# Writing the attention mask into PSUM with ScalarE, and moving the second half's scores

## The chip, the cores and the metric

The kernel runs on one core of one Trainium2 chip. The metric is device time in microseconds (us). The engines work from instruction streams of their own and meet at semaphores: TensorE (PE in the profile; its weight loads are PEld), VectorE (DVE), ScalarE (ACT), GpSimd (POOL), and SyncE (SP), which here only issues transfers (DMAs).

## The reference, cut to what matters

The program has four stages; the last one is six layers of local attention and a gated feed-forward net on 16 sequences of 256 tokens with 128 channels. The change concerns the scores of the local attention (16 heads, windows of 32 tokens, each of which sees its own window and the one before, so 64 keys):

```
mask = (it < jb) | (it > jb + w) | (jb == -1)
sim = einsum('bhwie,bhwje->bhwij', bq, bk2) * 8.0
sim = where(mask, -finfo.max, sim)
attn = softmax(sim, -1)
out = einsum('bhwij,bhwje->bhwie', attn, bv2)
```

In the kernel the banned places are 0 / -1e30 in a constant `mask_bf`, which the scores are added to.

## The kernel before, in words

The last stage (`phase_d_*`) runs 96 sequence-steps (6 layers by 16 sequences) as a software pipeline. Each engine has a hand-written loop over turns `f` (100 of them, `TURNS_D`), and each turn works on several sequences in different phases: sequence `f` is transposed, split and projected (chunks 0 to 4), `f-1` gets its chunks 5 to 7, its rotary products, norms and the placing of keys and queries, `f-2` its scores, softmax and token products, `f-3` the weighted sum (`attention`) and the start of the feed-forward net, `f-4` the rest of that net. The order on each engine is written out by hand; nothing is reordered.

The parts that matter here, by name and line:

- `scores(n, h)` on PE (L1915), once for each half `h` of a sequence, fills two PSUM banks, 2 and 3. For each bank it first puts the mask there by four products of `ident_bf` with `mask_bf` (L1923, one for each 32 rows, 512 columns, bf16), with `start=True`, and then adds 32 score products (L1930, `start=False`). It waits for the placed keys and queries (`s_dk`, `s_dq`) and for the subtraction that last read the banks (`s_sub`).
- On DVE `softmax_maximum` (L1470) and `softmax_shift` (L1476) read banks 2 and 3; the second signals `s_sub`. `rotary_products` (L1428) works on the projected chunks. `split_low_tokens` is L1416, `residual` L1503, `ffn_gate` L1529, `scale_keys` L1464.
- On ACT `squares` (L1660) reads each projected chunk, `softmax_exp` is L1676, `read_products` L1684, `ffn_gelu` L1723, and in three turns of each layer it also converts weights and makes tables (L1732, L1744, L1753).
- On POOL `rotary_sums` (L1815) adds the two rotary products, `add_halves` (L1823) adds squares, `scale_shifted` (L1832) scales the shifted scores, `softmax_scale` (L1838) the probabilities.
- On SP `place_queries` (L2141) and then `place_keys` (L2132) issue eight transfers each, SBUF to SBUF, for every sequence. The queries wait for the last rotary sum (`s_ad`), the keys for `scale_keys` (`s_mR`). The next sequence's first rotary sum waits until the keys have landed (`s_dk`, L1813), since it writes what they are read from.

PE's order in a turn: transpose tokens, up-projection of `f-4`, scores half 0, project 5, attention half 0, project 6, up-projection, project 7, scores half 1, `sum_squares` (L1901), attention half 1, token products (L1957) with projections 0 to 4 and the other work between them. The rings: a projected chunk's bank is free again when the rotary product two chunks back has been made (`s_rp`), and a rotary product's buffer when the rotary sum three chunks back is done (`s_ad`).

Of the kernel before, what the change touches and what calls it, by code (L numbers as in the profile page):

```python
# [20 lines left out]
ACT = mybir.ActivationFunctionType  # L21
# [50 lines left out]
def build(nc, dram, out):  # L72
    ctx = ExitStack()
    with ctx:
# [1094 lines left out]
        def phase_c_tensor(pe):  # L1169
# [86 lines left out]
            def sequence_turns(n, s, left):  # L1256
# [59 lines left out]
        tab_flat = tab[:, :, :, :, :].rearrange("p m k h t -> p (m k h t)")  # L1316
        base_stage = tab_flat[:, 4 * TPS * DH:4 * TPS * DH + 4 * TPS * P].rearrange("p (k t r f) -> p k t r f", k=4, t=TPS, r=4)

        (s_sel, s_basep, s_base, s_zk, s_normed, s_zero, s_stats, kept,
         s_xtp, s_xt, s_split, s_proj, s_sq, s_sa, s_xh, s_rp, s_ad, s_sm, s_y, s_r, s_zh, s_z, s_rq, s_R, s_mR, s_dk, s_dq,  # L1320
         s_s, s_sub, s_rm, s_exp, s_inv, s_prob, s_pt, s_u, s_uev, s_at, s_x2, s_x2p, s_xf, s_mean, s_xsq, s_var,
         d_chain, d_act_chain, s_y2, s_xc, s_xn, s_up, s_gl, s_h, s_ffo, s_x_done, s_m, s_mvo, s_whi, s_wlo, s_tab,
         loaded_qk, loaded_sc, loaded_vo, loaded_w1, loaded_w2) = (
            sem("d_" + s) for s in (
                "sel basep base zk normed zero stats kept "
                "xtp xt split proj sq sa xh rp ad sm y r zh z rq R mR dk dq "
                "s sub rm exp inv prob pt u uev at x2 x2p xf mean xsq var "
                "chain act_chain y2 xc xn up gl h ffo x_done m mvo whi wlo tab "
                "loaded_qk loaded_sc loaded_vo loaded_w1 loaded_w2").split())
        back = [sem(f"d_back{g}") for g in range(4)]  # L1330
        KEEP = NT // len(back)
        kept_in = wqk_stage[:, :].rearrange("p (g n c) -> p g n c", g=2, c=C)
        x_kept = [kept_in[:, 0], kept_in[:, 1], wvt[:, :, :], wo[:, :, :]]
        STORES = ((0, 4), (4, 8), (8, 12), (12, 15), (15, 16))
        ZEROS = 5
        TURNS_D = TOTAL + 4

        def at_least(eng, s, count):

            if count >= 1:  # L1340
                eng.wait_ge(s, count)
# [64 lines left out]
        def phase_d_vector(dve):  # L1406
# [116 lines left out]
            def ffn_gate(n, c):  # L1523
                if not here(n):
                    return
                m = FBLK[c]
                dve.wait_ge(s_gl, NF * n + c + 1)
                at_least(dve, s_ffo, n)
                nc.vector.scalar_tensor_tensor(d_h[0:m, c, :], bank[UP_BANK[c]][0:m, T:2 * T], cols_of(n)[0:m, 2 + c:3 + c],  # L1529
                                               d_gl[0:m, c % 2, :], ALU.add, ALU.mult).then_inc(s_h, 1)  # L1530
# [51 lines left out]
            for f in range(TURNS_D):  # L1582
                turn_probabilities(f - 3, 1)
                rotary_products(f - 1, 3)
                ffn_gate(f - 4, 0)
                rotary_products(f - 1, 4)
                softmax_maximum(f - 2, 0)
                rotary_products(f - 1, 5)
                softmax_shift(f - 2, 0)
                rotary_products(f - 1, 6, 7)  # L1590
                ffn_gate(f - 4, 1)
                softmax_maximum(f - 2, 1)
                split_low_tokens(f)
                ffn_gate(f - 4, 2)
                norm_weight(f - 1)
                residual(f - 3)
                norm_factor(f - 1)
                rotary_products(f, 0)
                norm_split(f - 1)
                softmax_shift(f - 2, 1)  # L1600
                scale_keys(f - 1, 0)
                rotary_products(f, 1)
                scale_keys(f - 1, 1)
                softmax_sum(f - 2, 0)
                rotary_products(f, 2)
                ffn_weight(f - 3)
                softmax_reciprocal(f - 2, 0)
                ffn_factor(f - 3)
                ffn_scale(f - 3)
                softmax_sum(f - 2, 1)  # L1610
                softmax_reciprocal(f - 2, 1)
                if f - 4 == LAST:
                    add_kept(3, SEQS - 4, SEQS - 1)
                ffn_residual(f - 4)
                turn_factors(f - 1)
                turn_probabilities(f - 2, 0)
                if f < 2:
                    normalise(*range(3 + 7 * f, min(10 + 7 * f, SEQS)))
                done = f - 4 - SEQS * (LAYERS - 1)
                if done > 0 and done % 4 == 0:  # L1620
                    add_kept(done // 4 - 1, done - 4, done)
# [3 lines left out]
        def phase_d_scalar(act):  # L1625
# [36 lines left out]
            def norm_rsqrt(n):  # L1662
                if not here(n):
                    return
                act.wait_ge(s_sm, 2 * n + 2)
                at_least(act, s_z, n)
                at_least(act, s_rq, n)
                link(nc.scalar.activation(d_y, bank[7][:, 0:T], ACT.Ln, bias=1e-24))
                link(nc.scalar.activation(d_y, d_y, ACT.Exp, scale=-0.5))
                nc.scalar.activation(d_w, d_y, ACT.Square).then_inc(s_y, 1)  # L1670

            def softmax_exp(n, h):
                if not here(n):
# [89 lines left out]
            for f in range(TURNS_D):  # L1763
                fresh = here(f) and f % SEQS == 0
                next_fresh = here(f + 1) and (f + 1) % SEQS == 0
                read_products(f - 3, 7)
                read_tokens(f)
                split_high_tokens(f)
                nc.scalar.preload_act_table(ACT.Gelu)
                ffn_gelu(f - 4, 0)  # L1770
                squares(f - 1, 5, 6)
                ffn_gelu(f - 4, 1)
                squares(f - 1, 7)
                ffn_gelu(f - 4, 2)
                nc.scalar.preload_act_table_set(EXP_SET)
                norm_rsqrt(f - 1)
                if fresh:
                    tables(layer_of(f), 0)
                softmax_exp(f - 2, 0)
                if here(f - 2) and (f - 2) % SEQS == 0:  # L1780
                    head_matrices(layer_of(f - 2))
                squares(f, 0)
                norm_high(f - 1)
                read_products(f - 2, 0, 1, 2)
                squares(f, 1)
                if fresh and f:
                    weights_high(layer_of(f), 4, 5, 6, 7)
                ffn_tokens(f - 3)
                read_products(f - 2, 3)
                ffn_square(f - 3)  # L1790
                read_products(f - 2, 4)
                squares(f, 2, 3)
                if fresh:
                    tables(layer_of(f), 1)
                if next_fresh:
                    weights_high(layer_of(f + 1), 0, 1, 2, 3)
                ffn_rsqrt(f - 3)
                softmax_exp(f - 2, 1)
                read_products(f - 2, 5)
                ffn_shift(f - 3)  # L1800
                squares(f, 4)
                read_products(f - 2, 6)


        def phase_d_gpsimd(pool):
# [32 lines left out]
                nc.gpsimd.tensor_tensor(d_e[h], d_e[h], d_inv[h].unsqueeze(2).to_broadcast([P, 4 * QUADS, 2 * WIN]), ALU.mult)\  # L1838
                    .then_inc(s_prob, 1)

            nc.gpsimd.memset(d_k, 0.0).then_inc(s_zk, 1)
            nc.gpsimd.memset(d_u[:, 0], 0.0).then_inc(s_zk, 1)
            for f in range(TURNS_D):
                fresh = here(f) and f and f % SEQS == 0
                next_fresh = here(f + 1) and (f + 1) % SEQS == 0
# [18 lines left out]
        def phase_d_tensor(pe):  # L1864
# [50 lines left out]
            def scores(n, h):  # L1915
                if not here(n):
                    return
                pe.wait_ge(s_dk, 128 * (n + 1))
                pe.wait_ge(s_dq, 128 * (n + 1))
                at_least(pe, s_sub, 2 * n + h)  # L1920
                for b in range(2):
                    for g in range(4):
                        nc.tensor.matmul(bank[2 + b][g * WIN:(g + 1) * WIN, :], ident_bf[:, g * WIN:(g + 1) * WIN],  # L1923
                                         mask_bf[:, min(h + b, 1), :, :].rearrange("p a k -> p (a k)"),
                                         start=True, stop=True, skip_group_check=True, tile_position=(0, g * WIN))
                    for v in range(2):
                        at = (4 * h + 2 * b + v) * WIN
                        for a in range(2):
                            for g in range(4):
                                last = nc.tensor.matmul(bank[2 + b][g * WIN:(g + 1) * WIN, (2 * v + a) * P:(2 * v + a + 1) * P],  # L1930
                                                        d_q[:, a, g, at:at + WIN], d_k[:, a, g, :, at:at + 2 * WIN],
                                                        start=False, stop=True, skip_group_check=True, tile_position=(0, g * WIN))
                last.then_inc(s_s, 1)
# [119 lines left out]
                last.then_inc(s_basep, 1)  # L2053
            pe.wait_ge(s_base, 4)
            pe.wait_ge(s_zero, ZEROS)
            pe.wait_ge(s_zk, 2)
            for f in range(TURNS_D):
                if f == 1:
                    pe.wait_ge(s_stats, 13)
# [6 lines left out]
                project(f - 1, 6)  # L2066
                ffn_up(f - 4, 2)
                project(f - 1, 7)
                scores(f - 2, 1)
                sum_squares(f - 1, 1)  # L2070
                attention(f - 3, 1)
                if here(f - 2) and (f - 2) % SEQS == 0:
                    head_matrices(layer_of(f - 2), 0, 1, 2, 3)
                token_products(f - 2, 0)
# [302 lines left out]
```

## Time and profile before

| | |
|---|---|
| runs | 4246.09 us median of 3 (4245.45 to 4252.16) |
| profiled execution | span 4245.4 us from the first to the last instruction, mean granted TensorE clock 0.965 |
| share of the span that each engine is busy | PE 92%, DVE 84%, ACT 62%, POOL 56% |
| last stage | about 1330 us to the end, 100 turns |
| two steady turns (PE's transposes of one turn to those of the next) | 29.21 us each |

The profile gives for the profiled execution its span; its own time is not listed apart from that. Busy shares are averages over four stages; the last stage has to be read by itself.

### The profile page before, as it was taken

Reading aid. Unit: us, or ns where it says so; the run is one execution under the profiler, and the core shown is the slowest. Engines: PE = TensorE matmul, PEld = TensorE weight load, DVE = VectorE, ACT = ScalarE, POOL = GpSimd, SP = SyncE. Lnnn points to the kernel's source line nnn. Section 1 sums busy time; section 2 is a strip of 40 time slices with the busy share of each in tenths; the row PEclk is TensorE's granted clock in tenths of the full one; section 3 lists DMA queues with packets and bytes.
Section 4 is the critical chain, followed back from the end, with each engine's and each line's share of the span. In section 5 each row is a group of like instructions: output and inputs, shape, how many; then the busy total and the mean of one; then the engine's idle time right before and its main releaser. Section 6 shows DMA issues by size and latency. Waiting matters only on the chain.

```text
span 4245.4 us, 120089 instructions
## 1 busy us (share of the span) xinstructions
PE 3898.6 (92%) x48128; PEld 2739.2 (65%) x48128; DVE 3566.7 (84%) x5529; ACT 2619.0 (62%) x5518; POOL 2380.4 (56%) x2045
## 2 busy tenths in 40 slices
PE   3457998999995999999999999999999999999998
PEld 1225776777774676667766676667766676667675
DVE  7986556777776899989998899989998899989897
ACT  2442335666664666666667666666666666666665
POOL 0111001000002787878888788878878787878785
PEclk7668999999997999999999999999999999999999
DMA  3000000000001333233332333233332333333332
GB/s 104 0 0 1 1 1 1 1 0 0 0 1 40 71 95 81 64 80 88 79 76 67 77 90 81 68 76 88 79 77 66 75 92 81 69 76 70 93 75 68
DMA packets 264482, 238.94 MB, mean 56 GB/s; under 512 B 31524, under 2 KB 260136, under 8 KB 263208
## 3 DMA queue, kind: packets, MB, share of 16 engines
q1 hardware_dynamic: 263976, 231.82, 23.4%
q8 instruction: 363, 5.95, 0.6%
q14 instruction: 143, 1.17, 0.1%
HBM read 26.20 MB, written 4.19 MB: 7 GB/s over the span
## 4 chain that ended last, share of the span: by engine, by line
PE 72%; DVE 13%; ACT 7%; issue 3%; SPq 2%; POOL 1%; DMA 1%; DVEq 0%; ACTq 0%; POOLq 0%
PE bank L1957 14%; PE bank L1890 13%; PE bank L1975 8%; PE bank L1930 7%; PE bank L2017 5%; PE bank L834 4%; ACT arena L1109 3%; PE bank L2030 2%; PE bank L1923 2%; DVE arena L996 2%; PE bank L1901 2%; DVE arena L1006 2%; PE bank L1234 1%; PE bank L1225 1%; PE bank L1912 1%
## 5 line engine op out<-in xcount | busy, mean ns | idle before, releaser
L1428 DVE TENSOR_TENSOR arena<-bank,tab 128x1024 f32<-128x1024 f32 x768 | 936.5, 1220 | 187.5 <-ACT arena L1660 136.0
L1815 POOL TENSOR_TENSOR arena<-arena 128x512 f32<-128x512 f32 x768 | 1009.8, 1330 | 47.4 <-DMA arena<-arena 43.2
L1660 ACT ACTIVATE arena<-bank 128x512 f32<-128x512 f32 x768 | 458.1, 597 | 537.8 <-PE bank L1890 527.8
L1957 PE MATMUL bank<-m_vo,arena 128*32 128x512 f32 x6144 | 757.6, 599 | 17.3 <-DVE arena L1521 11.0
L1890 PE MATMUL bank<-x_split,wqk_split 128*128 128x256 f32 x4608 | 720.1, 299 | 35.0 <-DVE arena L1428 21.0
L1890 PEld LDWEIGHTS bank<-x_split,wqk_split 128*128 128x128 f32 x4608 | 605.1, 191 | 183.9 <-issue 94.3
L1823 POOL TENSOR_TENSOR arena<-arena 128x256 f32<-128x256 f32 x768 | 556.7, 736 | 162.4 <-ACT arena L1660 161.9
L1684 ACT ACTIVATE arena<-bank 128x512 f32<-128x512 f32 x768 | 456.4, 595 | 187.4 <-PE bank L1957 184.7
L1832 POOL TENSOR_TENSOR arena<-arena 128x1024 f32<-128x1024 f32 x192 | 371.6, 1936 | 261.0 <-DVE arena L1476 261.0
L1167 POOL TENSOR_TENSOR x_all<-x_all,arena 128x256 f32<-128x256 f32 x16 | 11.6, 726 | 833.8 <-DVE arena L988 833.8
L1838 POOL TENSOR_TENSOR arena<-arena 128x1024 f32<-128x1024 f32 x192 | 373.4, 1945 | 127.3 <-DVE arena L1489 127.0
L1930 PE MATMUL bank<-arena 128*32 128x128 f32 x12288 | 403.0, 273 | 0.6 <-issue 0.6
L1975 PE MATMUL bank<-arena 128*32 128x128 f32 x12288 | 373.7, 274 | 0.0
L1930 PEld LDWEIGHTS bank<-arena 128*32 128x32 f32 x12288 | 345.1, 110 | 37.5 <-issue 1.2
L1975 PEld LDWEIGHTS bank<-arena 128*32 128x32 f32 x12288 | 333.1, 110 | 31.4 <-issue 0.7
L1957 PEld LDWEIGHTS bank<-m_vo,arena 128*32 128x32 f32 x6144 | 159.3, 109 | 260.2 <-ACT arena L1684 140.3
L1109 ACT ACTIVATE arena<-bank,arena 128x256 f32<-128x256 f32 x512 | 235.4, 472 | 131.0 <-DVE arena L996 130.0
L2017 PE MATMUL bank<-arena,w 128*128 128x256 f32 (+1 forms) x1152 | 280.7, 380 | 2.4 <-ACT arena L1715 2.0
L1496 DVE STREAM_TRANSPOSE arena<-arena 128x1024 f32<-128x1024 f32 x192 | 235.0, 1224 | 25.8 <-POOL arena L1838 25.8
L1470 DVE TENSOR_REDUCE arena<-bank 128x16 f32<-128x1024 f32 x192 | 234.2, 1220 | 12.1 <-PE bank L1930 4.1
L1464 DVE TENSOR_TENSOR arena<-arena,bank 128x1024 f32<-128x1024 f32 x192 | 232.4, 1210 | 2.1 <-PE bank L1912 2.1
L1476 DVE TENSOR_TENSOR arena<-bank,arena 128x1024 f32<-128x1024 f32 x192 | 233.5, 1216 | 0.0
(252 smaller groups left out, 7159.8 us busy)
## 6 DMA issues: line engine op xcount, KB each, us to landing
arena<-arena SPq DMA_DIRECT2D x1536, 128.0 KB, 2.5
wqk_stage<-in_wqk SPq DMA_DIRECT2D x6, 1024.0 KB, 8.5
out_x<-x_all SPq DMA_DIRECT2D x7, 512.0 KB, 6.0
wvt<-in_wvt SPq DMA_DIRECT2D x6, 512.0 KB, 4.4
wo<-in_wo SPq DMA_DIRECT2D x6, 512.0 KB, 5.5
arena<-in_wbh SPq DMA_DIRECT2D x1, 2048.0 KB, 9.6
w<-in_w SPq DMA_DIRECT2D x6, 341.0 KB, 5.7
wqk_stage<-out_x SPq DMA_DIRECT2D x2, 512.0 KB, 4.8
```

The source lines that it names most:

```text
L1428: nc.vector.tensor_tensor(d_t[c % KS].rearrange("p k h t -> p k (h t)"), bank[c % 2][:, :].unsqueeze(1).to_broadcast([P, 2, 2 * T]), tab[: ...
L1660: nc.scalar.activation(d_sq[i % 4].rearrange("p h t -> p (h t)"), bank[c % 2][:, :], ACT.Square).then_inc(s_sq, 1)
L1684: nc.scalar.activation(d_u[:, 1 + w, :, :], bank[U_BANK[w]][:, :].rearrange("p (a c) -> p a c", a=QUADS), ACT.Copy).then_inc(s_uev, 1)
L1815: nc.gpsimd.tensor_tensor(d_rot[i // 4][:, i % 4, :, :], t[:, :, 0, :], t[:, :, 1, :], ALU.add).then_inc(s_ad, 1)
L1823: nc.gpsimd.tensor_tensor(sq[:, 0, :], sq[:, 0, :], sq[:, 1, :], ALU.add).then_inc(s_sa, 1)
L1832: nc.gpsimd.tensor_tensor(e, e, factor.to_broadcast([P, WPT, QUADS, 2 * WIN]), ALU.mult).then_inc(s_rm, 1)
L1838: nc.gpsimd.tensor_tensor(d_e[h], d_e[h], d_inv[h].unsqueeze(2).to_broadcast([P, 4 * QUADS, 2 * WIN]), ALU.mult)\
L1890: last = nc.tensor.matmul(bank[c % 2][:, h * T:(h + 1) * T], wqk_split[:, i, wp, h, :], x_split[:, n % 2, xp, :], start=(q == 0), stop=(q ...
L1930: last = nc.tensor.matmul(bank[2 + b][g * WIN:(g + 1) * WIN, (2 * v + a) * P:(2 * v + a + 1) * P], d_q[:, a, g, at:at + WIN], d_k[:, a, g, ...
L1957: last = nc.tensor.matmul(bank[U_BANK[w]][g * WIN:(g + 1) * WIN, :], d_xt[n % 3][:, w * WIN:(w + 1) * WIN], m_vo[:, 4 * g:4 * g + 4, :].re ...
L1975: last = nc.tensor.matmul(bank[6][v * WIN:(v + 1) * WIN, h * C:(h + 1) * C], d_pt[h][:, at, :], d_u[:, WPT * h + v + z, r, :], start=(r == ...
L2017: last = nc.tensor.matmul(bank[UP_BANK[c]][0:m, half * T:(half + 1) * T], w1_of(n)[:, first + c * P:first + c * P + m], d_xn, start=True, ...
```

## The change

The mask is now put into banks 2 and 3 by one ScalarE copy for each half (`write_mask`, 128 x 1024, from `mask_bf`), which waits for the subtraction of the half before; the first half of the first sequence keeps the products. PE's `scores` waits for `s_mask` and issues only the score products. PE runs attention half 1 and `sum_squares` before scores half 1 (before: scores, `sum_squares`, attention). DVE does `softmax_maximum` of half 1 later, behind gate 2, the residual, the token split and the norm factor. A semaphore (`s_zk`) is merged into `s_zero`.

```diff
 # VectorE, in the turn
                 ffn_gate(f - 4, 1)
+                ffn_gate(f - 4, 2)
+                residual(f - 3)
+                split_low_tokens(f)
+                norm_weight(f - 1)
+                norm_factor(f - 1)
                 softmax_maximum(f - 2, 1)
-                split_low_tokens(f)
-                ffn_gate(f - 4, 2)
-                norm_weight(f - 1)
-                residual(f - 3)
-                norm_factor(f - 1)
 # ScalarE
+            def write_mask(n, h):
+                if not here(n) or n == 0 and h == 0:
+                    return
+                act.wait_ge(s_sub, 2 * n + h)
+                src = mask_bf[:, :, :, :] if h == 0 else mask_bf[:, 1:2, :, :].to_broadcast([P, TPS, 8, 2 * WIN])
+                nc.scalar.activation(psum[:, 2:4, :].rearrange("p b (a k) -> p b a k", k=2 * WIN), src, ACT.Copy).then_inc(s_mask, 1)
...
                 ffn_gelu(f - 4, 1)
+                write_mask(f - 2, 1)
                 squares(f - 1, 7)
...
                 softmax_exp(f - 2, 1)
+                write_mask(f - 1, 0)
                 read_products(f - 2, 5)
 # TensorE, scores
-                at_least(pe, s_sub, 2 * n + h)
+                if n == 0 and h == 0:
+                    for b in range(2):
+                        for g in range(4):
+                            nc.tensor.matmul(bank[2 + b][g * WIN:(g + 1) * WIN, :], ident_bf[:, g * WIN:(g + 1) * WIN],
+                                             mask_bf[:, min(h + b, 1), :, :].rearrange("p a k -> p (a k)"),
+                                             start=True, stop=True, skip_group_check=True, tile_position=(0, g * WIN))
+                else:
+                    pe.wait_ge(s_mask, 2 * n + h)
                 for b in range(2):
-                    for g in range(4):
-                        nc.tensor.matmul(bank[2 + b][g * WIN:(g + 1) * WIN, :], ident_bf[:, g * WIN:(g + 1) * WIN],
-                                         mask_bf[:, min(h + b, 1), :, :].rearrange("p a k -> p (a k)"),
-                                         start=True, stop=True, skip_group_check=True, tile_position=(0, g * WIN))
                     for v in range(2):
 # TensorE, in the turn
                 project(f - 1, 7)
+                attention(f - 3, 1)
+                sum_squares(f - 1, 1)
                 scores(f - 2, 1)
-                sum_squares(f - 1, 1)
-                attention(f - 3, 1)
 # GpSimd: the two memsets that signalled s_zk now signal s_zero (ZEROS 5 -> 7)
```

## Rows read from the trace of the kernel before

**Rows 1.** The page's part 1: busy us of each engine, share, instructions.

```profile
PE 3898.6 (92%) x48128; PEld 2739.2 (65%) x48128; DVE 3566.7 (84%) x5529; ACT 2619.0 (62%) x5518; POOL 2380.4 (56%) x2045
```

**Rows 2.** Windows view: stretch, length, busy us of each engine, clock, DMA share, GB/s.

```profile
2000.00:3700.00 1700.00, 1678.12 (x25060) 1182.16 (x25053) 1548.66 (x1886) 1153.51 (x2178) 1374.67 (x1173) 1.00 0.34 77
```

**Rows 3.** Timeline of PE: start, us, engine, line, operation, shapes.

```profile
2922.77 0.44 PE L1877 MATMUL bank<-ident,x_all 128*128 128x128 f32 x2
2924.87 0.40 PE L1923 MATMUL bank<-mask_bf,ident_bf 128*32 128x512 bf16 x4
2925.10 1.05 PE L1930 MATMUL bank<-arena 128*32 128x128 f32 x32
2925.97 0.39 PE L1923 MATMUL bank<-mask_bf,ident_bf 128*32 128x512 bf16 x4
...
2931.44 1.06 PE L1890 MATMUL bank<-x_split,wqk_split 128*128 128x256 f32 x6
2932.43 0.40 PE L1923 MATMUL bank<-mask_bf,ident_bf 128*32 128x512 bf16 x4
...
2951.98 0.44 PE L1877 MATMUL bank<-ident,x_all 128*128 128x128 f32 x2
```

**Rows 4.** Waits view: who waited for whom, us in total, times, longest.

```profile
POOL arena L1815 <- DMA arena<-arena: 43.2, 49, 5.2
...
PE bank L1890 <- DVE arena L1428: 21.0, 17, 5.2
```

**Rows 5.** Groups by form: line, operation, count, busy us, mean ns, idle before.

```profile
L1676 ACT ACTIVATE arena<-arena 128x1024 f32<-128x1024 f32 x192 | 201.7, 1050 | 47.2 <-POOL arena L1832 47.2
...
L1923 PE MATMUL bank<-mask_bf,ident_bf 128*32 128x512 bf16 x1536 | 151.8, 385 | 3.2 <-DMA arena<-arena 3.0 <-DVE arena L1476 0.2
```

**Rows 6.** Timeline of ACT, the same turn; in brackets idle before and releaser.

```profile
2932.54 0.60 ACT L1660 ACTIVATE arena<-bank 128x512 f32<-128x512 f32 x1 [0.61 <-PE bank L1890]
...
2937.12 1.06 ACT L1676 ACTIVATE arena<-arena 128x1024 f32<-128x1024 f32 x1 [0.53 <-POOL arena L1832]
2938.78 0.60 ACT L1660 ACTIVATE arena<-bank 128x512 f32<-128x512 f32 x1 [0.60 <-PE bank L1890]
...
2947.77 1.04 ACT L1676 ACTIVATE arena<-arena 128x1024 f32<-128x1024 f32 x1
2949.97 0.60 ACT L1684 ACTIVATE arena<-bank 128x512 f32<-128x512 f32 x1 [1.15 <-PE bank L1957]
```

**Rows 7.** Timeline of DVE, the same turn.

```profile
2925.73 1.23 DVE L1428 TENSOR_TENSOR arena<-bank,tab 128x1024 f32<-128x1024 f32 x1 [0.95 <-POOL arena L1815]
...
2930.65 1.22 DVE L1476 TENSOR_TENSOR arena<-bank,arena 128x1024 f32<-128x1024 f32 x1
...
2944.34 1.21 DVE L1464 TENSOR_TENSOR arena<-arena,bank 128x1024 f32<-128x1024 f32 x1
```

**Rows 8.** Timeline of POOL, the same turn and the next one's start.

```profile
2924.35 2.51 POOL L1815 TENSOR_TENSOR arena<-arena 128x512 f32<-128x512 f32 x2 [0.86 <-DMA arena<-arena]
...
2933.21 0.73 POOL L1823 TENSOR_TENSOR arena<-arena 128x256 f32<-128x256 f32 x1 [0.56 <-ACT arena L1660]
...
2937.05 2.90 POOL L1815 TENSOR_TENSOR arena<-arena 128x512 f32<-128x512 f32 x2
...
2952.72 2.52 POOL L1815 TENSOR_TENSOR arena<-arena 128x512 f32<-128x512 f32 x2
```

**Rows 9.** Timeline of SP: issue of keys (L2132) and queries (L2141).

```profile
2916.37 5.97 SPq L2132 DMA_DIRECT2D arena<-arena  x8
...
2939.98 5.12 SPq L2141 DMA_DIRECT2D arena<-arena  x8
2945.58 5.12 SPq L2132 DMA_DIRECT2D arena<-arena  x8
```

**Rows 10.** Timeline of ACT in a layer's first turn, near its end.

```profile
3244.64 1.04 ACT L1676 ACTIVATE arena<-arena 128x1024 f32<-128x1024 f32 x1
3245.58 0.58 ACT L1684 ACTIVATE arena<-bank 128x512 f32<-128x512 f32 x1
```

More of the change, by code:

```diff
@@ L1317, in build @@
         base_stage = tab_flat[:, 4 * TPS * DH:4 * TPS * DH + 4 * TPS * P].rearrange("p (k t r f) -> p k t r f", k=4, t=TPS, r=4)
-        (s_sel, s_basep, s_base, s_zk, s_normed, s_zero, s_stats, kept,
+        (s_sel, s_basep, s_base, s_normed, s_zero, s_stats, kept,
          s_xtp, s_xt, s_split, s_proj, s_sq, s_sa, s_xh, s_rp, s_ad, s_sm, s_y, s_r, s_zh, s_z, s_rq, s_R, s_mR, s_dk, s_dq,
          s_s, s_sub, s_rm, s_exp, s_inv, s_prob, s_pt, s_u, s_uev, s_at, s_x2, s_x2p, s_xf, s_mean, s_xsq, s_var,
-         d_chain, d_act_chain, s_y2, s_xc, s_xn, s_up, s_gl, s_h, s_ffo, s_x_done, s_m, s_mvo, s_whi, s_wlo, s_tab,
+         d_chain, d_act_chain, s_mask, s_y2, s_xc, s_xn, s_up, s_gl, s_h, s_ffo, s_x_done, s_m, s_mvo, s_whi, s_wlo, s_tab,
          loaded_qk, loaded_sc, loaded_vo, loaded_w1, loaded_w2) = (
             sem("d_" + s) for s in (
-                "sel basep base zk normed zero stats kept "
+                "sel basep base normed zero stats kept "
                 "xtp xt split proj sq sa xh rp ad sm y r zh z rq R mR dk dq "
                 "s sub rm exp inv prob pt u uev at x2 x2p xf mean xsq var "
-                "chain act_chain y2 xc xn up gl h ffo x_done m mvo whi wlo tab "
+                "chain act_chain mask y2 xc xn up gl h ffo x_done m mvo whi wlo tab "
                 "loaded_qk loaded_sc loaded_vo loaded_w1 loaded_w2").split())
@@ L1334, in build @@
         STORES = ((0, 4), (4, 8), (8, 12), (12, 15), (15, 16))
-        ZEROS = 5
+        ZEROS = 7
         TURNS_D = TOTAL + 4
@@ L1839, in softmax_scale @@
                     .then_inc(s_prob, 1)
-            nc.gpsimd.memset(d_k, 0.0).then_inc(s_zk, 1)
-            nc.gpsimd.memset(d_u[:, 0], 0.0).then_inc(s_zk, 1)
+            nc.gpsimd.memset(d_k, 0.0).then_inc(s_zero, 1)
+            nc.gpsimd.memset(d_u[:, 0], 0.0).then_inc(s_zero, 1)
             for f in range(TURNS_D):
@@ L2055, in phase_d_tensor @@
             pe.wait_ge(s_zero, ZEROS)
-            pe.wait_ge(s_zk, 2)
             for f in range(TURNS_D):
```

## The prediction, made before the changed kernel was run

> **What bounds the kernel now.** The first view is the page's list of busy times: PE is busy for 92% of the span, DVE for 84% [rows 1]. That is a mean over four stages, so next comes the windows view of the last stage alone. From 2000 to 3700 us PE is busy 1678 of 1700 us at full clock (1.00, the 2.4 GHz level), DVE 1549, POOL 1375, ACT 1154 [rows 2]. PE is the bound there, DVE has some 9% of air, ACT 32%. Third, PE's timeline: its turns start at 2922.77 and 2951.98, 29.21 us apart [rows 3]. Of the 95 such distances in the stage 65 are 29.20 to 29.22, whatever the other engines do; about 17 belong to turns in which a layer begins (30.3, 31.7 and about 34 us), the rest are up to 0.8 us longer or the filling of the pipeline. So an ordinary turn costs what PE has to issue. Last, the waits view: POOL's first rotary sum waited 49 times, 43.2 us in all, for the keys' transfers, and PE's projection 17 times, 21.0 us, for a rotary product [rows 4]. These say which chain stands right behind PE.
>
> **What goes off PE.** Each turn has two halves with two banks, so four groups of four mask products. The group that starts at 2924.87 is followed by the scores at 2925.10; the next one starts 0.87 us after that, and the others repeat this to 0.01 [rows 3]. A group thus costs 0.22 to 0.23 us of PE's time, although each product is listed with 385 ns [rows 5]: four run side by side, and the listed end overlaps the scores. Four groups are 0.89 us a turn. The busy total, 151.8 us [rows 5], would be 1.58 us a turn; I leave it out as an end, since the starts show that the scores run under it. The ordinary turn becomes 29.21 - 0.89 = 28.32 us if PE stays the bound. Moving scores half 1 behind attention half 1 and `sum_squares` adds nothing to PE: the same instructions in another order. I price it at nothing. It gives time for the mask: scores half 1 start at about 11.4 us into the turn, while the mask is ready at 9.8 (below), so the new wait is covered by 1.6 us. Behind that wait stand the token products and all that follows on PE; without the cover each us of it is a us of the turn.
>
> **What comes onto ACT.** Two copies of 128 x 1024 a turn. No row shows ACT writing PSUM from a bf16 source. Nearest is the softmax exponential, same size, 1050 ns [rows 5]; two squares of 128x512 out of PSUM would be 2 x 0.60 = 1.20 [rows 6], the upper end; the lower end is 0.84, the exponential without a fixed part (slope between it and the 0.42 us instructions of 256 elements that the ACT timeline has). I take 1.05 with about 0.95 until the next instruction starts, since neighbours overlap by 0.1. The Trainium skill, "ScalarE: Activation LUTs", section "Step-by-step: what each stage is for", says that PSUM is the lower-latency port for a ScalarE destination; no row here shows it. By that the copy would be no dearer than the exponential, and nothing below changes by more than 0.1 us a turn.
>
> The write of half 0 stands behind the second exponential. That starts at 2947.77, and the next ACT instruction waits 1.15 us for PE afterwards [rows 6]; the copy's 0.95 goes into that hole. Cost: nothing in an ordinary turn, up to 0.95 us in the turns that begin a layer, where the hole is full (exponential at 3244.64, next instruction at 3245.58) [rows 10].
>
> The write of half 1 is the one with a price. It stands ahead of `squares` of chunk 7 and waits for the first subtraction. Count from the keys' landing r (the first rotary sum of the turn starts then, or when POOL is free). The sum starts at 2924.35, the rotary product that it frees at 2925.73, the subtraction at 2930.65 [rows 7, 8], ending 1.22 later: r + 7.52. The copy takes 0.95 plus some 0.04 for the semaphore, so the square starts at r + 8.5. Before, it started at 2932.54 = 9.77 into the turn, when PE had projected [rows 3, 6]; with two mask groups gone that would be 9.32. ACT's queue behind the copy holds that square, the third gelu, the table load, the norms, the exponential. The square ends 0.67 later and POOL goes on at r + 9.17 (before: 2933.21), which leads after 3.91 us to the exponential (2937.12) and after 6.77 to SP's queries (2939.98) [rows 6, 8, 9]. ACT can then take the first square of the next sequence at r + 9.17 + 3.91 + 0.95 = r + 14.03. PE offers it at 2938.78 - 2922.77 = 16.01 before and 15.12 after [rows 3, 6]. So PE is held up as soon as r exceeds 1.09 us. A second way of saying it: projection 5 needs the rotary product that ends at r + 2.6, and PE wants it at 3.9: the same threshold within 0.3. Before, r was 1.58 in this turn and 0.74 in the next [rows 3, 8], and no turn suffered.
>
> **Does r get smaller?** No. The keys can't be issued before the queries: SP needs 5.12 us for eight and 5.60 lay between first query and first key [rows 9], of which 0.4 was waiting for `scale_keys` (started 2944.34, ended 2945.55 [rows 7]); the least is 5.2. From a first key's issue to the next turn's rotary sum it took 7.98 us (2916.37 to 2924.35) and less than 7.1 (2945.58 to 2952.72, no wait on it) [rows 8, 9]. The two kinds alternate nearly turn by turn; 49 late ones waited 0.88 us each on the mean [rows 4], so a late landing takes 8.0. The loop is r + 9.17 + 6.77 + 0.03 + 5.2 = r + 21.17, then 7.03 or 8.0: 28.2 or 29.2 us around, mean 28.7, against 28.32 for PE. From r = 1.09, a late landing gives 1.09 + 21.17 + 8.0 - 28.32 = 1.94, or 0.85 us of hold-up; the early one after it gives about 1.0, no hold-up. Mean 0.43. About a quarter of the query issues take 0.3 to 1 us more than 5.12; the 0.4 of slack that took them before is gone: another 0.12. The turn becomes 28.32 + 0.43 + 0.12 = 28.87.
>
> **DVE.** Nothing is added. The chain from its rotary product 7 (now 10.3 into the turn) to `scale_keys` half 1 is 11.6 us of back-to-back work, ending at 21.9, ahead of the 22.3 at which SP is free for keys. Maximum half 1 in its new place starts at 14.5, when scores half 1 are done since 13.2. The token split ends at 13.9 for a projection at 14.1: covered by 0.2 only, and late together with r, so it is part of the same hold-up.
>
> **Sum.** 29.21 - 28.87 = 0.34 us in 78 ordinary turns = 27 us. In the 17 layer-beginning turns I take 0: 0.89 comes off PE, 0.95 to 1.9 goes onto a full ACT. The set-up (semaphore merged, eight products kept) is nothing. The profiled span is 4245.4 us and the runs' median 4246.1, so the span stands for the median: 4246 - 27 = 4219 us.
>
> **Rivals.** (B) PE stays the bound: landings come early enough, or SP and POOL run ahead. For it: 65 turns at exactly PE's price. Against: r was 1.58 without harm only because the threshold lay higher. Gain 0.89 x 78 = 69, with half of it in the layer-beginning turns 77: 4169 to 4177 us. The Trainium skill, "PSUM — Partial Sum Buffer", section "Engine vs sequencer instructions", says that ScalarE's queue is strictly first in, first out; ACT's timeline agrees, being the written order with idle before squares whose operand is late (0.61 us) [rows 6]. If the square could pass the waiting copy, the loop would lose 0.8 us and B would be the forecast; the rule speaks against it.
> (C) The hold-up eats all: landings are late in every turn. The turn is 28.32 + 0.85 + 0.12 = 29.29, within 0.1 of now: 4246 + 6 = 4252, or no change where it is a little less.
> (D) Slower: the write of half 1 keeps ACT from its square. It decides once copy and its wait take over 0.35 us more than I have them (the copy above 1.4 us). At 1.9 us: 28.87 + 0.85 = 29.72, + 0.51 x 78 = 40, and 1 us for each of 17 special turns: 4303. At 1.5 us about 4265.
> (E) The change doesn't do what it says (scores without mask, or PE waits in place of the products): the wait has 1.6 us of cover; 4% at most, inside C.
>
> **Numbers.** Forecast 0.42 (its own range 4200 to 4236), B 0.28, C and E 0.17, D 0.13. What a measurement can tell from no change is 0.2%, 8.5 us: faster needs under 4237.6. Forecast and B nearly all count as faster, and some of C comes out just below: 0.72; same 0.15, slower 0.13. The range leaves out the far part of D and what lies beyond B: 4162 to 4256.
>
> **What would show it.** In the changed profile: no L1923 after the first half; a copy of about 1.05 us twice a turn on ACT, idle before one of them with DVE's subtraction named; PE's turns not at one value but alternating between about 28.3 and 29.2, with PE's idle put down to ACT or DVE at the token products or projections; POOL's wait for the DMA still some 50 times or more. All turns at 28.3 would be B. All above 29.2, with squares idle behind the copy, would be D. The forecast fails if the landings no longer alternate, or if the copy's duration is off by more than 0.3 us.

## The result and the profile after

The changed kernel takes 4294.95 us (median of 4, 4293.87 to 4296.53) against 4245.77 us: ratio 1.0115, 95% interval 1.0103 to 1.0127. It is slower by 49 us. The prediction was 4219 us in a range of 4162 to 4256, so it was wrong in size and in sign. Every run below is compared with the kernel before as it was run beside it (4245.6 to 4247.2 us).

The page's first line, its part 1 and its chain by engine, kernel after:

```profile
span 4292.7 us, 117223 instructions
PE 3865.7 (90%) x46600; PEld 2693.8 (63%) x46600; DVE 3672.3 (86%) x5529; ACT 2790.0 (65%) x5709; POOL 2398.6 (56%) x2045
DVE 33%; PE 30%; issue 16%; ACT 8%; SPq 5%; POOL 4%; DMA 3%; DVEq 0%; ACTq 0%; POOLq 0%
```

The work did what it was to do on PE: 1528 matmuls fewer. But VectorE has the same 5529 instructions and is busy for 3672 us in place of 3567 [rows 1]: 106 us more for unchanged work. The third line is the chain that ended last, by engine: now DVE leads. In the kernel before PE had it:

```profile
PE 72%; DVE 13%; ACT 7%; issue 3%; SPq 2%; POOL 1%; DMA 1%; DVEq 0%; ACTq 0%; POOLq 0%
```

The windows view of the same stretch as [rows 2]:

```profile
2000.00:3700.00 1700.00, 1634.95 (x23658) 1134.99 (x23650) 1586.15 (x1854) 1236.13 (x2257) 1358.78 (x1148) 1.00 0.33 76
```

DVE has 37 us more of work and PE 43 us less in 1700 us. The ordinary turn, here and below the most frequent distance between PE's transposes of one turn and the next, went from 29.21 to 29.70 us (3122.26 to 3151.96); 40 of the stage's 95 distances are 29.69 to 29.71. Most of the others are longer, so a mean is given too where it matters: over the 70 turns that neither fill the pipeline nor stand at a layer's beginning it went from 29.33 to 29.93 us. Which VectorE instructions grew is seen when lines are asked one by one (min/median/max ns); the first two rows are of before, the last two of after:

```profile
L1416 DVE TENSOR_TENSOR x_split<-arena,x_split x96: 424/1352/1361, 1329.1 to 4155.9; 128x256 fp32r<-128x256 f32 x96
L1442 DVE SCALAR_TENSOR_TENSOR arena<-arena x96: 442/458/1565, 1355.6 to 4186.4; 128x256 f32<-128x256 f32 x96
```

```profile
L1416 DVE TENSOR_TENSOR x_split<-arena,x_split x96: 424/2129/2142, 1325.8 to 4200.8; 128x256 fp32r<-128x256 f32 x96
L1442 DVE SCALAR_TENSOR_TENSOR arena<-arena x96: 425/1065/1076, 1352.3 to 4231.5; 128x256 f32<-128x256 f32 x96
```

The token split grew by 0.78 us and the norm factor by 0.61 us, 1.39 us a turn. Summed over the stage they grew by 126 us, and no other line of VectorE changed by more than 5 us. Both read two operands from SBUF. The timelines of DVE and POOL around them, kernel after:

```profile
3132.54 1.23 DVE L1428 TENSOR_TENSOR arena<-bank,tab 128x1024 f32<-128x1024 f32 x1 [0.48 <-ACT arena L1660]
3134.46 0.41 DVE L1503 TENSOR_TENSOR x_all<-x_all,bank 128x256 f32<-128x256 f32 x1
3134.79 2.12 DVE L1416 TENSOR_TENSOR x_split<-arena,x_split 128x256 fp32r<-128x256 f32 x1
3136.84 0.41 DVE L1436 SCALAR_TENSOR_TENSOR arena<-bank,arena 128x256 f32<-128x256 f32 x1
3137.28 1.07 DVE L1442 SCALAR_TENSOR_TENSOR arena<-arena 128x256 f32<-128x256 f32 x1
3138.27 1.21 DVE L1470 TENSOR_REDUCE arena<-bank 128x16 f32<-128x1024 f32 x1
...
3134.52 2.12 POOL L1841 TENSOR_TENSOR arena<-arena 128x1024 f32<-128x1024 f32 x1
3136.60 2.90 POOL L1824 TENSOR_TENSOR arena<-arena 128x512 f32<-128x512 f32 x2
```

The split starts at 3134.79, 0.27 us into GpSimd's scaling, which ends at 3136.64; the split ends at 3136.91, 0.27 later by these rounded rows. The factor ends at 3138.35, 0.28 after the first of the two rotary sums (3138.07). Matched over the stage, 95 of the 96 splits, in this kernel and in the kernel before alike, end 0.28 or 0.29 us after the end of the GpSimd instruction that ran when they started; the first split met no GpSimd instruction and took 0.424 us. In the kernel before, the split started 0.86 us into the same scaling and the factor 1.30 us into the rotary sum, so both were held less (DVE and POOL, kernel before):

```profile
2936.01 1.35 DVE L1416 TENSOR_TENSOR x_split<-arena,x_split 128x256 fp32r<-128x256 f32 x1
2938.02 0.40 DVE L1503 TENSOR_TENSOR x_all<-x_all,bank 128x256 f32<-128x256 f32 x1
2938.35 0.46 DVE L1442 SCALAR_TENSOR_TENSOR arena<-arena 128x256 f32<-128x256 f32 x1
...
2935.16 1.93 POOL L1832 TENSOR_TENSOR arena<-arena 128x1024 f32<-128x1024 f32 x1
```

The neighbours of the same size with one operand in PSUM (L1503, L1436) take 0.40 to 0.43 us in both kernels. The Trainium skill has this on the page "SBUF — State Buffer", section "Who interferes with whom": VectorE and GpSimd share a pair of ports that is locked by one of them at a time, a VectorE instruction with two SBUF inputs contends with a GpSimd instruction that reads SBUF, and the order of issue decides which of them waits. The trace agrees in both kernels: the split that starts after GpSimd's scaling ends 0.28 us behind it. Such waiting inside an instruction is called a hold below.

The new copy, the wait and PE's scores were as forecast. Timelines of ACT and PE, kernel after:

```profile
3130.55 0.47 ACT L1730 ACTIVATE arena<-bank,cols_d 128x256 f32<-128x256 f32 x1
3130.96 1.03 ACT L1677 ACTIVATE bank<-mask_bf 128x1024 f32<-128x1024 bf16 x1
3131.92 0.58 ACT L1660 ACTIVATE arena<-bank 128x512 f32<-128x512 f32 x1
...
3133.82 1.93 PE L1942 MATMUL bank<-arena 128*32 128x128 f32 x64
3136.97 1.70 PE L1899 MATMUL bank<-x_split,wqk_split 128*128 128x256 f32 x12 [0.36 <-DVE x_split L1416]
3147.94 0.95 PE L1899 MATMUL bank<-x_split,wqk_split 128*128 128x256 f32 x6 [0.43 <-DVE arena L1428]
```

The mask is written by 3131.99 and the scores start at 3133.82: 1.8 us of cover. PE waits for the split and for a rotary product that comes after it.

### The profile page after: what moved, and what is told of

It reads as the page before. It is cut to its first block, busy times and chain, and to the rows that moved or that the text cites. A ratio compares the mean times of both kernels' runs of the same rounds, so it can differ in the third digit from the quotient of the medians.

```text
span 4292.7 us, 117223 instructions
## 1 busy us (share of the span) xinstructions
PE 3865.7 (90%) x46600; PEld 2693.8 (63%) x46600; DVE 3672.3 (86%) x5529; ACT 2790.0 (65%) x5709; POOL 2398.6 (56%) x2045
## 4 chain that ended last, share of the span: by engine, by line
DVE 33%; PE 30%; issue 16%; ACT 8%; SPq 5%; POOL 4%; DMA 3%; DVEq 0%; ACTq 0%; POOLq 0%
DVE arena L1428 5%; PE bank L834 4%; DVE arena L1464 4%; PE bank L1899 4%; PE bank L1969 4%; SPq L2143 4%; DVE x_split L1416 4%; ACT arena L1109 3%; DMA arena<-arena 3%; PE bank L1987 2%; PE bank L1942 2%; POOL arena L1824 2%; PE bank L2029 2%; DVE arena L1476 2%; DVE arena L996 2%
## 5 line engine op out<-in xcount | busy, mean ns | idle before, releaser
L1841 POOL TENSOR_TENSOR arena<-arena 128x1024 f32<-128x1024 f32 x192 | 389.2, 2027 | 298.8 <-DVE arena L1476 298.8
L1167 POOL TENSOR_TENSOR x_all<-x_all,arena 128x256 f32<-128x256 f32 x16 | 11.6, 727 | 833.1 <-DVE arena L988 833.1
L1847 POOL TENSOR_TENSOR arena<-arena 128x1024 f32<-128x1024 f32 x192 | 373.5, 1946 | 130.7 <-DVE arena L1489 130.7
L1942 PE MATMUL bank<-arena 128*32 128x128 f32 x12288 | 375.6, 274 | 1.8 <-DMA arena<-arena 1.6
L1987 PE MATMUL bank<-arena 128*32 128x128 f32 x12288 | 376.7, 275 | 0.0
L1942 PEld LDWEIGHTS bank<-arena 128*32 128x32 f32 x12288 | 335.7, 110 | 51.0 <-issue 32.1
L1987 PEld LDWEIGHTS bank<-arena 128*32 128x32 f32 x12288 | 324.8, 110 | 26.6 <-issue 1.3
L1683 ACT ACTIVATE arena<-arena 128x1024 f32<-128x1024 f32 x192 | 201.7, 1051 | 108.9 <-POOL arena L1841 108.9
```

The lines of the kernel that those rows point to most:

```text
L1841: nc.gpsimd.tensor_tensor(e, e, factor.to_broadcast([P, WPT, QUADS, 2 * WIN]), ALU.mult).then_inc(s_rm, 1)
L1987: last = nc.tensor.matmul(bank[6][v * WIN:(v + 1) * WIN, h * C:(h + 1) * C], d_pt[h][:, at, :], d_u[:, WPT * h + v + z, r, :], start=(r == ...
```

## The experiments

Two theories. P: the loss is VectorE being held by GpSimd, brought about by the new order. Q: the loss is the copy in ScalarE's queue ahead of a square, the prediction's case D.

**e1, mask by ScalarE, both orders as before.**

```diff
 # after.py, TensorE
+                scores(f - 2, 1)
+                sum_squares(f - 1, 1)
                 attention(f - 3, 1)
-                sum_squares(f - 1, 1)
-                scores(f - 2, 1)
 # and VectorE's six calls in the order of before
```

> The mask by ScalarE alone, the orders on TensorE and VectorE as in the kernel before. Two theories of the 49 us. Theory P (VectorE waits for GpSimd): in the changed kernel the token split and the norm factor, VectorE instructions whose two inputs both lie in SBUF, now start early in a GpSimd instruction and end 0.27 us after that one ends: 2.12 instead of 1.35 us and 1.07 instead of 0.46 us, and VectorE has become the bound. With the order of before the split is 1.2 to 1.5 us and the factor under 0.6 us; TensorE waits up to 0.9 us for the mask ahead of the second half's scores; turn 28.6 to 29.2 us, time 4200 to 4245. Theory Q (ScalarE's queue): the copy that stands ahead of the square of chunk 7 delays GpSimd and the loop over the keys; it does so here too: turn 29.5 to 29.8, time 4275 to 4300.

Measured: 4248.93 us against 4246.64, ratio 1.0007 (0.9998 to 1.0017): the same. Ordinary turns 29.01 us, but only 27 of 70 are near it and their mean is 29.33, as in the kernel before; split 1.45, factor 0.46 us. PE waits for the mask in the waits view of 2000 to 3700 us:

```profile
PE bank L1942 <- ACT bank L1677: 34.6, 58, 0.7
```

That is 0.6 us a turn out of the 0.89 won; what takes the rest in the longer turns was not followed. The time is 4 us above P's range (4245) and far from Q's. The copy ahead of the square is present here and costs no 49 us: Q alone is not the cause.

**e2, the two orders alone, mask by products.**

```diff
 # before.py, TensorE
-                scores(f - 2, 1)
-                sum_squares(f - 1, 1)
                 attention(f - 3, 1)
+                sum_squares(f - 1, 1)
+                scores(f - 2, 1)
 # and VectorE's six calls in the order of after
```

> Only the two orders of the changed kernel (TensorE and VectorE), the mask by products as before. Theory P: the split again falls early into GpSimd's 1.93 us instruction (about 1.9 to 2.1 us) and the factor into the next (about 1 us), VectorE's work is 28 us or more a turn; with TensorE at 29.2 the turn is 29.2 to 29.5, time 4246 to 4275. Theory Q: no copy, so no cost: TensorE stays the bound, turn 29.21, time 4246 within 5 us, and the split's length does not matter.

Measured: 4290.36 us, ratio 1.0105 (1.0088 to 1.0122). The orders alone cost 44 us, ordinary turns 29.83; the mean of the 70, 29.94, is that of the changed kernel (29.93). Split and factor:

```profile
L1416 DVE TENSOR_TENSOR x_split<-arena,x_split x96: 425/2126/2139, 1327.0 to 4195.3; 128x256 fp32r<-128x256 f32 x96
L1442 DVE SCALAR_TENSOR_TENSOR arena<-arena x96: 426/1065/1073, 1354.2 to 4226.2; 128x256 f32<-128x256 f32 x96
```

Both as long as in the changed kernel without any copy. The time is above P's range (4275), the direction is P's; Q expected no cost.

**e3, the changed kernel, mask behind the square.**

```diff
-                write_mask(f - 2, 1)
                 squares(f - 1, 7)
+                write_mask(f - 2, 1)
```

> The changed kernel with the second half's mask written behind the square of chunk 7 instead of ahead of it. The square then starts 0.5 to 0.9 us earlier, and GpSimd's next instructions with it; the scores of the second half still find the mask there. Theory Q: the whole loss goes, turn 28.4 to 28.9, time 4170 to 4215. Theory P: GpSimd's long instruction ends 0.5 to 0.9 us earlier, so the split is shorter by as much (1.2 to 1.6 us), turn 29.0 to 29.4: 4235 to 4270.

Measured: 4265.82 us, ratio to before 1.0047 (1.003 to 1.0063), ordinary turns 29.42. The time lies in P's range, but its reason was wrong: the split stayed at 2.13 us (median 2125 ns), again 0.28 us into the scaling (DVE, then POOL):

```profile
3119.18 2.13 DVE L1416 TENSOR_TENSOR x_split<-arena,x_split 128x256 fp32r<-128x256 f32 x1
...
3118.90 2.12 POOL L1841 TENSOR_TENSOR arena<-arena 128x1024 f32<-128x1024 f32 x1
```

The square releases VectorE's rotary product 7 and GpSimd's next instruction alike, so both moved together and the split met the scaling at the same point. So the place of the copy is worth 29 us in the changed kernel, through the square, beside the holds. The prices found by e2, e3 and e4 (44, 29 and 91 us) were each measured in another surrounding and don't add up to the 49.

**e4, the changed kernel, split moved on VectorE.**

```diff
-                rotary_products(f - 1, 6, 7)
+                rotary_products(f - 1, 6)
+                split_low_tokens(f)
+                rotary_products(f - 1, 7)
...
                 residual(f - 3)
-                split_low_tokens(f)
```

> The changed kernel with the token split moved on VectorE to between the rotary products 6 and 7, where VectorE waits 0.48 us for the square and GpSimd is idle for 1.1 us. Theory P: the split takes 0.4 to 0.7 us instead of 2.12, VectorE's work falls by 1.2 to 1.7 us a turn, the turn to 28.4 to 29.1 us, time 4170 to 4240; the norm factor is still held by GpSimd. Theory Q: the split isn't on the way, the copy still is: turn 29.5 to 29.7, time 4275 to 4295.

Measured: 4204.07 us, ratio 0.9893 (0.9874 to 0.9913). Ordinary turns 28.50. The split:

```profile
L1416 DVE TENSOR_TENSOR x_split<-arena,x_split x96: 410/415/562, 1329.3 to 4111.8; 128x256 fp32r<-128x256 f32 x96
```

95 of the 96 splits now start while GpSimd is idle. The same instruction takes 0.42 us there, and the changed kernel is 91 us faster for it.

**e5, the split with one SBUF input, in its place.** Its second operand is read from a PSUM bank (another low part is computed; the diff has the call alone).

```diff
-tensor_tensor(x_split[:, n % 2, 1, :], d_xt[n % 3], x_split[:, n % 2, 0, :].bitcast(F32), ALU.subtract)
+tensor_tensor(x_split[:, n % 2, 1, :], d_xt[n % 3], bank[6][:, 0:T], ALU.subtract)
```

> The changed kernel, orders untouched; the token split (VectorE) reads its second input from PSUM bank 6 instead of from SBUF, so that only one input lies in SBUF. It computes another low part, so the projections are wrong; size, place and output are the same. If an instruction with two SBUF inputs is held until GpSimd's running one ends, this one isn't held: about 0.42 us in place of 2.12 at the same place, beside the same GpSimd instruction. The norm factor stays two-input and is held instead, about 0.9 to 1.1 us. VectorE gains 1.4 to 1.7 us a turn, the turn falls from 29.70 to 28.3 to 28.8, time 4175 to 4220. If the length comes from something else (the fp32r output, the place in the order), the split stays at 2.1 us or so and the turn at 29.7.

Measured: 4204.3 us, ratio 0.9904 (0.9887 to 0.9921), ordinary turns 28.50. Timelines of DVE and POOL:

```profile
3138.72 0.41 DVE L1416 TENSOR_TENSOR x_split<-arena,bank 128x256 fp32r<-128x256 f32 x1
3139.88 0.80 DVE L1442 SCALAR_TENSOR_TENSOR arena<-arena 128x256 f32<-128x256 f32 x1
...
3138.45 1.95 POOL L1841 TENSOR_TENSOR arena<-arena 128x1024 f32<-128x1024 f32 x1
```

Again 0.27 us into the scaling, again an fp32r output, and 0.41 us long. It is the second SBUF input that holds it, and neither the output's type nor the place. The factor, still with two, ends at 3140.68, 0.28 after the scaling; its 0.80 us are below the 0.9 to 1.1 expected. The scaling itself is back from 2.12 to 1.94 us (median).

**e6, the changed kernel, norm factor with one input in PSUM.**

```diff
-scalar_tensor_tensor(d_w, bank[7][:, 0:T], 1e-24, d_w, ALU.max, ALU.mult)
+scalar_tensor_tensor(bank[7][:, T:2 * T], bank[7][:, 0:T], 1e-24, d_w, ALU.max, ALU.mult)
-scalar_tensor_tensor(d_y, d_w, 3.0, d_y, ALU.subtract, ALU.mult)
+scalar_tensor_tensor(d_y, bank[7][:, T:2 * T], 3.0, d_y, ALU.subtract, ALU.mult)
```

> The changed kernel; the norm's product goes through the free half of PSUM bank 7, so the norm factor (VectorE) has one SBUF input and one in PSUM. Same result. Expected by the hold theory: the factor 0.40 to 0.46 us instead of 1.07, the split still 2.12, the turn 0.5 to 0.65 us shorter than 29.70, 29.05 to 29.25: time 4235 to 4255. If VectorE's length in this place isn't what sets the turn: 29.7, 4295.

Measured: 4248.07 us, ratio 1.0003 (0.9994 to 1.0013). The factor:

```profile
L1442 DVE SCALAR_TENSOR_TENSOR arena<-bank,arena x96: 424/425/427, 1353.4 to 4180.6; 128x256 f32<-128x256 f32 x96
```

The split is still 2.13, ordinary turns are 29.07: the 0.64 us come off the turn nearly one for one.

**e7 and e8, both repairs, then also the mask behind the square** (the diffs of e4 and e6, then of e3).

> Both repairs on the changed kernel: the split between the rotary products 6 and 7, and the norm factor with one input in PSUM. Split 0.42, factor 0.42. VectorE is then at about 26 us of work a turn and TensorE is the bound again, at 29.21 - 0.89 = 28.32, with the hold-ups of the keys' landing in some turns: ordinary turns 28.3 to 28.5, time 4180 to 4200. If the loop over the keys with the copy in ScalarE's queue is what stands at 28.5, no gain over the split alone (4204).

> The same as the one before with the second half's mask written behind the square of chunk 7. The square, GpSimd and the keys come earlier: less hold-up by late keys. Turns at 28.3 more often, time 4165 to 4190. If the copy ahead of the square cost nothing, as the one before within 3 us.

Measured: e7 4200.98 us, 0.9894 (0.9877 to 0.991), ordinary turns 28.50; e8 4183.63 us, 0.985 (0.9833 to 0.9866), ordinary turns 28.40. With the split moved, the factor's repair adds 3 us, which the intervals of e4 and e7 don't tell from nothing (e7 was expected at 4200 at most): VectorE is no longer what binds. The copy ahead of the square then stands for 17 us. 15 of them lie in the 70 turns, whose mean goes from 28.79 to 28.57: the common turn is 0.1 us shorter, and fewer turns are longer than it. e8 is the fastest kernel of the study. Its windows row:

```profile
2000.00:3700.00 1700.00, 1668.04 (x24534) 1180.81 (x24534) 1517.59 (x1928) 1291.57 (x2359) 1383.90 (x1200) 1.00 0.34 79
```

PE is busy for 98% again, at more turns in the same time.

**e9, the changed kernel with VectorE's order of before** (TensorE's order new; the six calls of VectorE put back).

> The changed kernel with VectorE's order of before: the maximum of the second half ahead of the split, the gate, the norms and the residual. TensorE keeps its new order, so the maximum waits for scores that end later. By the changed kernel's trace: gate 1 at 3133.7, scores done at 3135.75, so VectorE idles 1.3 us or more, then maximum, then a split that starts at 36.9 and is held by GpSimd's rotary sum to 38.3: 0.4 to 1.0 us a turn more than the changed kernel, time 4320 to 4375. If VectorE's new order is itself the whole cause of the loss, this kernel is faster than the changed one, 4245 to 4260.

Measured: 4348.35 us, ratio 1.0244 (1.0227 to 1.0261), ordinary turns 29.97. Timeline of DVE:

```profile
3138.27 0.47 DVE L1529 SCALAR_TENSOR_TENSOR arena<-bank,cols_d,arena 128x256 f32<-128x256 f32 x1
3140.41 1.23 DVE L1470 TENSOR_REDUCE arena<-bank 128x16 f32<-128x1024 f32 x1 [1.67 <-PE bank L1942]
3141.55 1.00 DVE L1416 TENSOR_TENSOR x_split<-arena,x_split 128x256 fp32r<-128x256 f32 x1
```

VectorE idles 1.67 us for the scores. Its new order was thus needed once PE's was changed, and better by 53 us than leaving it; it is the split's place in it that costs.

**e10 and e11, the repairs without the mask's change**: on the kernel before, and on the two new orders with the mask by products.

> The kernel before with the two repairs alone: split between the rotary products 6 and 7, norm factor with one input in PSUM. VectorE's work falls by about 1 us a turn, but TensorE is the bound at 29.21: the ordinary turns stay at 29.21, time 4235 to 4248. A clear gain of more than 0.5% would mean that the turns of before weren't TensorE's price after all.

> The two new orders with both repairs, the mask by products. If the orders cost only through VectorE's held instructions, nothing is left of their 44 us: ordinary turns 29.2 to 29.3, time 4235 to 4255; and the gain of the kernel with both repairs and the mask by ScalarE (4201; 4184 with the mask behind the square) is the products' price, 0.7 to 0.8 us a turn. If moving the scores costs something of its own, this stays above 4265.

Measured: e10 4245.1 us, 0.9994 (0.9984 to 1.0004), ordinary turns 29.20; e11 4244.02 us, 0.9998 (0.9988 to 1.0007), ordinary turns 29.23. In the kernel before the held split costs nothing, since PE is the bound. And the orders cost nothing once the holds are gone: their 44 us are the holds. What is left between e11 and e8, 60 us and 0.83 us a turn, is the mask's products taken off PE; with the copy where the change has it (e11 to e7) it is 43 us.

## Why the prediction was wrong, step by step

- **PE's saving** was forecast at 0.89 us a turn and a bound of 28.32. e8's ordinary turns are 28.40 against 29.23 with the products (e11): 0.83. Right. Counting starts and not the listed 385 ns [rows 3, 5] was what made it so.
- **The copy** was forecast at 1.05 us, 0.95 in the queue, and took 1.02, 0.96 (3130.96 to 3131.92). Its own wait, mask to scores, was covered by 1.8 us (forecast 1.6). Right. Case D, a copy above 1.4 us, was the wrong way to the right sign.
- **"Nothing is added" on DVE, and its chain from rotary product 7 to `scale_keys` half 1 "is 11.6 us of back-to-back work, ending at 21.9"**: this is the step that failed. It ends at 3145.53, 23.27 into the turn. The 1.37 us between are the 1.39 us by which split and factor grew. I took durations from the trace as fixed, while these two depend on where in a GpSimd instruction they start. The sum for the path to the token split said 13.9 with 0.2 us of cover; it ended at 14.65, and PE waited 0.36 us for it.
- **Moving scores half 1 on PE, "I price it at nothing"**, was right of PE's own instructions only. The move of PE's order forced VectorE's (e9), and that moved the split by 0.6 us against GpSimd. e2 gives the price, 44 us, and e11 shows that it is only the holds.
- **The loop over the keys** was forecast as what stands behind PE: a mean hold-up of 0.55 us, turns alternating between 28.3 and 29.2. In the changed kernel the turns are 29.70 and don't alternate; the keys are issued when `scale_keys` ends and not when SP is free of the queries (3144.64), as the timelines of DVE and SP in the kernel after show:

```profile
3144.33 1.20 DVE L1464 TENSOR_TENSOR arena<-arena,bank 128x1024 f32<-128x1024 f32 x1
...
3139.52 5.12 SPq L2152 DMA_DIRECT2D arena<-arena  x8
3145.56 5.11 SPq L2143 DMA_DIRECT2D arena<-arena  x8
```

  e7 is the kernel to judge the hold-up by, since the copy stands there as in the forecast and VectorE doesn't bind. The mean of its 70 turns is 28.79 us, 0.47 above 28.32, so the size was about right; e8, with the copy behind the square, still has 0.25 of it. GpSimd's first rotary sum waited for transfers 51 times, as against 49 before [rows 4]:

```profile
POOL arena L1825 <- DMA arena<-arena: 43.0, 51, 5.7
```

  The pattern was wrong: half of these turns are 28.50 and the others go up to 29.5 without alternating. Which part of it the copy causes through this loop, and which by another path, is settled by no run; its place is worth the 17 us between e7 and e8.
- **The sum itself** would have been too small even without the holds: e7 is 46 us faster than the kernel before beside it, the forecast said 27. It set 28.87, a mean, against 29.21, the common turn, while the mean before was 29.33; and it took the turns at a layer's beginning at nothing, where e7 gains 7 us. (Its early landing of 7.03 us is 7.14 by the rows, at most 0.06 us a turn.)
- **What the trace of before would have told**: the split's 1.35 us beside 0.40 us for a residual of the same 128x256 with one operand in PSUM, and 0.424 us for the first split, when GpSimd was idle. An instruction three times as long as its equal beside it was waiting here, though no wait was listed.

## What to carry to other kernels

Before moving a VectorE instruction with two SBUF inputs, look at what GpSimd runs at that moment in the trace: here the split, 0.42 us alone, ended 0.28 us after GpSimd's running instruction whatever that one's length, and most of its listed 2.13 us was a wait in disguise. Put such instructions where GpSimd idles (e4), or give one operand to PSUM (e5, e6); on a kernel that another engine bounds, this gains nothing until that engine's work is cut (e10 against e8). When an order is changed on the bound engine to win time, price the order that the next engine must then take, not only the moved instructions.

## What the runs showed of the hardware that was not expected

- A VectorE instruction of 128x256 with two SBUF inputs takes 0.42 us alone and up to 2.14 us beside GpSimd (the split), ending 0.28 or 0.29 us after GpSimd's instruction in 95 of 96 cases, in the kernel before as in the changed one. With one input in PSUM it takes 0.41 us beside the same GpSimd instruction (e5).
- The held time counts as busy: VectorE's 86% in the changed kernel contains about 1.7 us of holding per turn in the split alone (2.13 against 0.42), so a busy share is no measure of VectorE's work while GpSimd runs.
- The holding costs GpSimd something too. Its scaling took 2.12 us (median) in the four kernels in which a split with two SBUF inputs started 0.27 or 0.28 us into it (after, e2, e3, e6), and 1.94 us in e5, where the split started at the same point with one. In the kernel before, with the split 0.86 us into it, the scaling took 1.93.
- ScalarE writes 128x1024 fp32 into two PSUM banks from a bf16 source in 1.02 us, against 1.05 us for the exponential of the same size from SBUF to SBUF.
